# Extra multiplications on TensorE between the phases, and each phase's ScalarE function evaluated once at its head

## The chip, the cores and the metric

The kernel runs on one core of a Trainium2 chip. The metric is the device time of one execution in microseconds: 2099.31 us is the median of three runs before the change (2096.52 to 2101.40).

## The reference

x has 8 batches of 512 tokens with 256 features, all in fp32. Three layers are applied one after the other, each added to x:

```python
x = x + 0.5 * ffn(layernorm(x))
x = x + attn(layernorm(x))
x = x + 0.5 * ffn(layernorm(x))

def ffn(x):                      # the same weights both times
    gf = global_net(mean(x, axis=tokens))       # 256 -> 128 -> 64 -> 1, gelu, gelu, sigmoid
    out = x
    for _ in range(3):
        tf = coupling_net(out)                  # 256 -> 256 -> 128 -> 64 -> 1, three gelu, sigmoid
        coupling = 0.1 + adaptive_range * (0.7 * gf + 0.3 * tf - 0.5) * 2
        out = out + coupling * twist(out)       # [o, p] -> [p, -p, -o, o], by quarters
    return out

def attn(x):                     # 16 heads of 64, and 4 memory keys and values
    q, k, v = x @ Wq, x @ Wk, x @ Wv            # q and k normalised per head
    dots = W_pre_th mixed over heads of (q k^T * 10), causal
    dots = the 64 largest of each row kept, the rest masked
    attn = W_post_th mixed over heads of softmax(dots)
    return (attn @ v * head_scale * sigmoid(x @ Wg + bg)) @ Wo
```

## The kernel before

The program has three phases, each a block in which every engine runs its own list of instructions; the engines meet at the end of a block. Between attention and the second ffn phase stands a fourth part that recomputes a batch if a check asks for it; in this execution it is skipped, and only its flag is read.

**The ffn phase** (`ffn_phase`, L77) runs twice, first with `setup` (it also loads and prepares the weights and makes the identity matrix on GpSimd, L611 and L613), then without it. Its state is kept transposed in SBUF. For each of the 8 batches x is loaded (a DMA on ScalarE's queue in the first phase, L415, on SyncE's in the second, L171 and L175), VectorE normalises it into `xn` (L199 to L214, with GpSimd's power at L277), TensorE turns it with eight transposes (`turn_in`, L285), and ScalarE copies it into the state (`take_in`, L389). Then TensorE works through 24 units (3 cycles of 8 batches) in a loop over 27 steps (L327), in which step k does the first layer of unit k (L342), the second of unit k-1 (L354), and for a pair of units the third (L363) and fourth (L373). `turn_in(k + 2)` stands inside the loop in the first steps. ScalarE evaluates Gelu and Tanh between them, and VectorE updates the state (`update`, four instructions) and at the end adds half of the turned state to x (`add_back`, L248). The state is turned back by `turn_back(b)` (L294, eight transposes at L300); those of batches 0 to 4 stand in the loop, those of 5 to 7 behind it (L380). Each waits for the update of its batch and for the PSUM pair that add_back of batch b-2 frees. In the first phase TensorE then turns the memory keys (`turn_memory`, L711). When add_back of a batch is done SyncE stores the batch, and it waits for all stores before the block ends.

**Attention** (`attention_phase`, L728) treats 32 tiles of 128 tokens, each in 16 groups of 8 rows. Its order on TensorE is written out by hand (L1126 to L1191): `xT(0)` turns the normalised first tile, `tokens` projects q and k (L1008, four calls each), `turn_qk` turns q and then k (L1031), `score` makes the scores (L1049), which ScalarE copies to SC and a DMA brings into `raw`; then the loop over pairs of groups begins with `mix(0)` (L1060) and, for the next tile, `xT(1)` and its q. Before `turn_qk` q and k are squared and copied by ScalarE (L1211, L1214), summed by VectorE (L1525), raised to the power -1/2 by GpSimd (L1411) and scaled by VectorE (L1532). The first `exp` (L1310) comes behind the first steps of that loop.

Every engine's instructions run in the order of the list, and a wait holds back all that stands behind it on that engine.

Of the kernel before, what the change touches and what calls it, by code (L numbers as in the profile page):

```python
# [7 lines left out]
ACT = mybir.ActivationFunctionType  # L8
# [5 lines left out]
P = 128  # L14
# [54 lines left out]
    return -z, step / 2, -step * (counted / 2 - wanted)  # L69


def tiles_of(dram, b):

    return dram[b * N:(b + 1) * N, :].rearrange("(t p) d -> p t d", p=P)


def ffn_phase(nc, tag, X, W, x_dram, out_dram, setup=None, ahead=(), reload=()):  # L77


    with ExitStack() as c:  # L80
        def sb(name, shape):
            return c.enter_context(nc.sbuf_tensor(f"{tag}_{name}", shape, F32))
# [9 lines left out]
        ST = sb("state", [P, 2, B, N])  # L92
        xsum = sb("xsum", [P, 2, B])
        g1 = sb("g1", [P, B])
        g2 = sb("g2", [64, B])
        gth = sb("gth", [P, B])
        offs = sb("offs", [P, B])
# [9 lines left out]
        bank3 = c.enter_context(nc.psum_tensor(f"{tag}_bank3", [P, 512], F32))  # L107
# [175 lines left out]
        def _(pe):  # L283

            def turn_in(b):  # L285
                pe.wait_ge(xn_ready, b + 1)
                wide_free(pe, "x", b)
                for half in range(2):
                    for t in range(TPB):
                        last = nc.tensor.transpose(wide("x", b)[:, half, t * P:(t + 1) * P],  # L290
                                                   xn[b % 2][:, t, half * P:(half + 1) * P], W.ident[:, :])
                last.then_inc(xn_turned, 1)

            def turn_back(b):  # L294
                pe.wait_ge(upd_done, NU - B + b + 1)
                wide_free(pe, "back", b)
                for t in range(TPB):
                    for half in range(2):
                        at = t % 2 * D + half * P
                        last = nc.tensor.transpose(wide("back", b)[:, t // 2, at:at + P],  # L300
                                                   ST[:, half, b, t * P:(t + 1) * P], W.ident[:, :])
                last.then_inc(back_turned, 1)
# [15 lines left out]

            if setup:
                pe.wait_ge(setup.ident_made, 2)  # L320
            turn_in(0)
            turn_in(1)
            if setup:
                pe.wait_ge(setup.ffn_in, 16 * setup.ffn_loads)
# [2 lines left out]
            for k in range(STEPS):  # L327
# [17 lines left out]
                if 0 <= k - 1 < NU:  # L345
# [7 lines left out]
                    for kk in range(2):  # L353
                        last = nc.tensor.matmul(bank2[:, :], W.cn_w2[:, kk, :], h1[u % 2][:, kk, :], start=kk == 0,  # L354
                                                stop=kk == 1)
# [22 lines left out]
                if 0 <= k - (NU - 2) < B:  # L378
                    turn_back(k - (NU - 2))
            for b in range(STEPS - NU + 2, B):  # L380
                turn_back(b)
            if setup:
                pe.wait_ge(h2_ready, NU)
                setup.turn_memory(pe, bank2)

        @block.scalar
        def _(act):

            def take_in(b):  # L389
                act.wait_ge(xn_turned, b + 1)  # L390
                for half in range(2):
                    nc.scalar.activation(ST[:, half, b, :], wide("x", b)[:, half, :], ACT.Identity,
                                         accum_out=xsum[:, half, b:b + 1]).then_inc(state_in, 1)

            def context(h, piece):
                cols = slice(QUAD * h, QUAD * h + QUAD)
                dst, rows, w_bias, scale, func = ((g1, P, W.gc_b1, 1.0 / N, ACT.Gelu), (g2, 64, W.gc_b2, 1.0, ACT.Gelu),
                                                  (gth, P, W.gc_b3h, 0.5, ACT.Tanh))[piece]
                act.wait_ge(g_mm, 3 * h + piece + 1)
                nc.scalar.activation(dst[0:rows, cols], bank2[0:rows, 0:QUAD], func, bias=w_bias[0:rows, 0:1],  # L400
                                     scale=scale).then_inc(g_act, 1)

            def coefficients(pair):
                act.wait_ge(tf_ready, pair + 1)
                act.wait_ge(offs_ready, 1 if 2 * pair % B < QUAD else 2)
                if pair >= 2:
                    act.wait_ge(upd_done, 2 * pair - 2)
                for i in range(2):
                    b = (2 * pair + i) % B
                    nc.scalar.activation(cs[pair % 2][:, i, :], tf[pair % 2][:, i, :], ACT.Identity,  # L410
                                         bias=offs[:, b:b + 1], scale=W.sgn_ar03[:, 0:1]).then_inc(cs_ready, 1)

            if setup:
                for b in range(B):
                    act.dma_start(X[:, b * TPB:(b + 1) * TPB, :], tiles_of(setup.x, b)).then_inc(x_loaded[part_of[b]], 16)  # L415
                setup.store_zeros(act)
            take_in(0)
            take_in(1)
            if setup:
                act.wait_ge(setup.ffn_in, 16 * setup.ffn_loads)  # L420
            for k in range(STEPS):
                if k in G_STEPS:
                    if k == 3 and setup:
                        act.wait_ge(setup.ffn_built, setup.ffn_builds)
                    context(*G_STEPS[k])
                if k < NU:
                    u = k
                    if u >= 2:
                        act.wait_ge(w2_done, u - 1)
                    for m in range(2):  # L430
                        act.wait_ge(w1_done, 2 * u + m + 1)
                        nc.scalar.activation(h1[u % 2][:, m, :], wide("w1", u)[:, m, :], ACT.Gelu,
                                             bias=W.cn_b1[:, m:m + 1]).then_inc(h1_ready, 1)
                if 0 <= k - 1 < NU:
                    u = k - 1
                    if u >= 4:
                        act.wait_ge(w3_done, (u - 4) // 2 + 1)
                    act.wait_ge(w2_done, u + 1)
                    nc.scalar.activation(h2[u % 4][:, :], bank2[:, :], ACT.Gelu, bias=W.cn_b2[:, 0:1]).then_inc(h2_ready, 1)
                if 0 <= k - 2 < NU and k % 2:  # L440
                    pair = (k - 2) // 2
                    if pair >= 2:
                        act.wait_ge(w4_done, pair - 1)
                    act.wait_ge(w3_done, pair + 1)
                    nc.scalar.activation(h3[pair % 2][:, :], bank3[:, :], ACT.Gelu, bias=W.cn_b3[:, 0:1]).then_inc(h3_ready, 1)
                if 0 <= k - 3 < NU and k % 2 == 0:
                    pair = (k - 3) // 2
                    if pair >= 2:
                        act.wait_ge(cs_ready, 2 * pair - 2)
                    act.wait_ge(w4_done, pair + 1)  # L450
                    nc.scalar.activation(tf[pair % 2][:, :, :], pair_out[:, :, :], ACT.Tanh, bias=W.cn_b4h[:, 0:1],  # L451
                                         scale=0.5).then_inc(tf_ready, 1)
                    if pair >= B // 2 - 1:
                        coefficients(pair)
                if k % 2 and 0 <= (k - 5) // 2 < B // 2 - 1:
                    coefficients((k - 5) // 2)
                if k + 2 < B:
                    take_in(k + 2)
            if setup:
                setup.keep_memory(act, bank2)  # L460
# [267 lines left out]
def attention_phase(nc, W, token_weights, a, x_dram, out_dram, again):  # L728

    with ExitStack() as c:  # L730
        def sb(name, shape, dtype=F32):
            return c.enter_context(nc.sbuf_tensor(name, shape, dtype))
# [31 lines left out]
        minus_thr = sb("minus_thr", [P, RING])  # L764
        below = sb("below", [P, RING])
        signs = sb("signs", [P, RING])
        side = sb("side", [P, RING])
        order = sb("order", [P, RING])
        flip = sb("flip", [P, RING], I32)
# [220 lines left out]
        def _(pe):  # L990

            def xT(j):
                def emit():
                    for k in range(2):
                        last = nc.tensor.transpose(bankD[:, 0, k * P:(k + 1) * P], xn[:, k * P:(k + 1) * P], W.ident[:, :])
                    return last
                pe.wait_ge(xn_ready, j + 1)
                pe_use(pe, ("xT", j, 0), emit)
# [116 lines left out]
            def project(t):  # L1115
# [7 lines left out]
                                            stop=q == PAIRS - 1)  # L1123
                last.then_inc(projected, 1)

            xT(0)  # L1126
            tokens(0, "q", Wq)
            tokens(0, "k", Wk)
            turn_qk(0, 0, "qT")
            turn_qk(0, 1, "kT")  # L1130
            for q in range(4):
                score(0, q)
            for n0 in range(0, NG + LAG, 2):
                t, g = divmod(n0, GPT)
                live, ahead = n0 < NG, t + 1 < NT
# [58 lines left out]
        def _(act):  # L1194

            def xT(j):
                if j >= 2:

                    wait_read(act, ("g", j - 2, 1))
                act_use(act, ("xT", j, 0), lambda: nc.scalar.copy(  # L1200
                    xnT[j % 2][:, :, MEM:MEM + P], bankD[:, 0, 0:D].rearrange("p (k n) -> p k n", k=2)))
# [111 lines left out]
            def out_PT(n0):  # L1313
# [14 lines left out]
                    last = nc.scalar.copy(PTtail[0:MEM, :, :], bankT[0:MEM, 0:P].rearrange("p (h i) -> p h i", i=IG))  # L1328
                last.then_inc(PT_out, 2)

            xT(0)
            project_qk(0, 0, "q")
            project_qk(0, 1, "k")
# [1287 lines left out]
```

## Time and profile before

| what | value |
|---|---|
| median of three runs | 2099.31 us |
| the profiled execution | 2098.69 us |
| its span | 2096.9 us |
| mean granted TensorE clock | 0.981 |
| first ffn phase | 0 to about 202 us |
| attention | about 202 to 1894 us |
| second ffn phase | about 1897 us to the end |

In the profile times are microseconds unless marked ns. PE is TensorE's multiplication, PEld its weight load, DVE VectorE, ACT ScalarE, POOL GpSimd, SPq and ACTq the DMA queues of SyncE and ScalarE. L300 is line 300 of the kernel before. PEclk is the granted TensorE clock, in tenths on the page and as a share of full speed in a table of stretches. "x8" counts the records merged into one row. A multiplication is pipelined and its end modelled, so a row can reach a little over the start of the next.

### The profile page before, as it was taken

How to read it: one execution, taken by the hardware profiler on the slowest of the kernel's cores; microseconds unless marked ns; L12 is line 12 of the kernel's file. 1: busy time of each engine (PE TensorE's matmuls, PEld its weight loads, DVE VectorE, ACT ScalarE, POOL GpSimd, SP SyncE). 2: the span in 40 equal slices, each digit the busy share in tenths (PEclk: the TensorE clock that was granted, in tenths of full speed). 3: DMA queues.
4: the chain of work that ended last, by engine and by line, in shares of the span. 5: the costliest groups of instructions: out<-in, count | busy, mean ns of one | idle time of the engine just before them, and what ended most of it. 6: DMA issues, size and time to landing. Idle time of an engine off the chain costs nothing. (4 is left out here: it accounts for less than half of the span.)

```text
span 2096.9 us, 56133 instructions
## 1 busy us (share of the span) xinstructions
PE 1952.4 (93%) x16059; PEld 1292.3 (62%) x16060; DVE 1668.8 (80%) x7716; ACT 1612.7 (77%) x4412; POOL 862.8 (41%) x2675
## 2 busy tenths in 40 slices
PE   7996789999999999999999999999999999996997
PEld 3433456676667666766676677666766776674433
DVE  6355389978997899789978997999699969985335
ACT  4553489978997899789968996899689978963554
POOL 3000454455445544554454445544554455421000
PEclk9997899999999999999999999999999999998998
DMA  5002012301230222122211221122112211213002
GB/s 170 26 1 95 12 33 53 79 18 45 61 73 18 62 55 60 26 54 68 45 33 48 68 48 29 48 68 48 29 48 68 48 26 46 66 45 95 0 1 80
DMA packets 113228, 104.78 MB, mean 50 GB/s; under 512 B 34449, under 2 KB 110865, under 8 KB 112913
## 3 DMA queue, kind: packets, MB, share of 16 engines
q1 hardware_dynamic: 108000, 96.65, 18.6%
q10 hardware_dynamic: 4912, 4.46, 0.7%
q8 instruction: 134, 2.20, 0.5%
q14 instruction: 182, 1.48, 0.2%
HBM read 19.14 MB, written 12.71 MB: 15 GB/s over the span
## 5 line engine op out<-in xcount | busy, mean ns | idle before, releaser
L1076 PEld LDWEIGHTS bankC<-R,E 128*128 128x128 f32 x2560 | 319.9, 192 | 49.7 <-issue 17.6
L1060 PE MATMUL bankB<-raw,mixpre 128*128 128x76 f32 (+37 forms) x1024 | 334.5, 421 | 13.6 <-DMA raw<-SC 12.3
L1076 PE MATMUL bankC<-R,E 128*128 128x128 f32 x2560 | 333.9, 277 | 11.5 <-POOL R L1452 11.5
L1557 DVE TENSOR_SCALAR_CACHE_REDUCE S<-S,minus_thr 128x68 f32<-128x68 f32 (+56 forms) x456 | 232.9, 511 | 110.9 <-POOL minus_thr L1436 110.1
L1427 POOL TENSOR_TENSOR S<-S,diagmask 128x8 f32<-128x8 f32 x512 | 120.2, 238 | 395.4 <-ACT S L1284 360.4
L1284 ACT ACTIVATE S<-bankB,aim_first 128x68 f32<-128x68 f32 (+56 forms) x456 | 227.3, 506 | 57.8 <-PE bankB L1060 56.9
L1452 POOL TENSOR_SCALAR R<-mixpost,rinv 128x128 f32<-128x128 f32 x512 | 199.3, 402 | 101.1 <-DVE rinv L1591 99.0
L1310 ACT ACTIVATE E<-S,nmax 128x12 f32<-128x12 f32 (+56 forms) x512 | 238.8, 523 | 0.0
L1060 PEld LDWEIGHTS bankB<-raw,mixpre 128*128 128x128 f32 x1024 | 160.2, 190 | 119.0 <-issue 94.4
L1646 DVE SCALAR_TENSOR_TENSOR E<-S,limit,E 128x68 f32<-128x68 f32 (+56 forms) x456 | 221.8, 521 | 8.6 <-ACT E L1310 4.7
L1049 PE MATMUL bankD<-KT,QT 64*64 64x132 f32 (+8 forms) x2304 | 177.4, 401 | 43.3 <-ACT qk L1214 29.4
L1102 PEld LDWEIGHTS bankM<-PT,V 128*64 128x64 f32 x5120 | 176.2, 138 | 65.2 <-issue 61.8
L1102 PE MATMUL bankM<-PT,V 128*64 128x64 f32 x5120 | 199.4, 226 | 1.2 <-ACT PTtail L1328 1.2
L1320 ACT COPY PT<-bankC 128x256 f32<-128x256 f32 (+3 forms) x256 | 175.1, 684 | 31.4 <-PE bankT L1082 18.2
L1302 ACT ACTIVATE junk_side<-S 128x68 bf16<-128x68 f32 (+56 forms) x456 | 198.6, 443 | 0.0
L1294 ACT ACTIVATE junk_first<-S 128x60 bf16<-128x60 f32 (+56 forms) x456 | 196.3, 440 | 0.2
L1411 POOL TENSOR_TENSOR rn<-ssq,neghalf 128x16 f32<-128x16 f32 x64 | 190.0, 2969 | 11.3 <-DVE ssq L1526 10.5
L1602 DVE TENSOR_SCALAR near<-S,flip 128x68 int32<-128x68 int32 (+56 forms) x456 | 158.3, 387 | 0.1
L238 DVE TENSOR_TENSOR ffn_mo<-ffn_cs,ffn_state 128x512 f32<-128x512 f32 x48 | 32.9, 686 | 139.3 <-ACT ffn_cs L410 139.3
L1273 ACT COPY SC<-bankD 128x520 f32<-128x520 f32 (+4 forms) x160 | 128.5, 803 | 9.5 <-PE bankD L1049 7.3
L1049 PEld LDWEIGHTS bankD<-KT,QT 64*64 64x64 f32 x2304 | 59.5, 133 | 109.8 <-ACT SC L1273 44.7
L1008 PE MATMUL bankD<-Wq,xnT 128*128 128x512 f32 x256 | 121.8, 620 | 5.0 <-ACT xnT L1200 5.0
(187 smaller groups left out, 4188.7 us busy)
## 6 DMA issues: line engine op xcount, KB each, us to landing
X_first<-in_L_attn_x_dram ACTq DMA_DIRECT2D x8, 512.0 KB, 9.9
x<-X_first SPq DMA_DIRECT2D x8, 512.0 KB, 2.9
xt<-x SPq DMA_DIRECT2D x32, 128.0 KB, 2.4
x<-xt SPq DMA_DIRECT2D x32, 128.0 KB, 2.4
X_last<-x SPq DMA_DIRECT2D x8, 512.0 KB, 7.5
out_dram<-X_last SPq DMA_DIRECT2D x8, 512.0 KB, 2.9
raw<-SC SPq DMA_DIRECT2D x8, 258.0 KB, 5.3
raw<-SC SPq DMA_DIRECT2D x8, 254.0 KB, 4.8
```

The source lines that it names most:

```text
L1049: last = nc.tensor.matmul(bankD[cols, r, i * s[3]:(i + 1) * s[3]], QT[rows, pair, HALF * hh:HALF * hh + HALF], KT[rows, pair, first:first ...
L1060: last = nc.tensor.matmul(bankB[n % 2][:, 0:wide(n)], W.mixpre[:, :], raw[n % RAWS][:, 0:wide(n)], start=True, stop=True)
L1076: last = nc.tensor.matmul(bankC[:, n % 2, jb * P:(jb + 1) * P], E[n % EBUFS][:, jb * P:(jb + 1) * P], R[n % RBUFS][:, :], start=True, stop ...
L1102: last = nc.tensor.matmul(bankM[64 * lo:64 * lo + 64, pair * HALF:(pair + 1) * HALF], V[:, slot(t - blocks + 1 + jb), h * DH:(h + 1) * DH] ...
L1284: nc.scalar.activation(S[n % SBUFS][:, 0:wide(n)], src, ACT.Identity, bias=W.aim_first[:, group(n)]).then_inc(S_out, 1)
L1294: nc.scalar.activation(junk_first[n % 2][:, 0:w], S[n % SBUFS][:, 0:w], ACT.Sign, scale=-1.0, accum_out=below[:, col(n)]).then_inc(below_d ...
L1302: nc.scalar.activation(junk_side[n % 2][:, 0:w], S[n % SBUFS][:, 0:w], ACT.Sign, accum_out=signs[:, col(n)]).then_inc(signs_done, 1)
L1310: nc.scalar.activation(E[n % EBUFS][:, 0:w], S[n % SBUFS][:, 0:w], ACT.Exp, bias=nmax[:, col(n)]) \
L1411: nc.gpsimd.tensor_tensor(rn[:, i, :], ssq[:, i, :], W.neghalf[:, 0:H], ALU.pow).then_inc(rn_ready, 1)
L1452: nc.gpsimd.tensor_scalar(R[n % RBUFS][:, :], W.mixpost[:, :], rinv[:, col(n)], 1.0, ALU.mult, ALU.mult).then_inc(R_ready, 1)
L1557: nc.vector.tensor_scalar(row, row, minus_thr[:, col(n)], None, ALU.add, ALU.max, accum_out=rmax[:, col(n)]).then_inc(max_done, 1)
L1646: at[n] = step(nc.vector.scalar_tensor_tensor(out=E[n % EBUFS][:, 0:w], in0=S[n % SBUFS][:, 0:w], scalar=least, in1=E[n % EBUFS][:, 0:w], ...
```

## The change

A helper `keep_busy(nc, W, bank, times)` is added. It issues `times` multiplications whose weights are the identity matrix (128x128) and whose moving operand is the identity repeated four times (128x512), into a PSUM bank that nothing reads at that point. None of them waits for anything or signals anything. It is called

- in each ffn phase ahead of `turn_in(0)` (7 times in the first, 9 in the second), ahead of `turn_in(1)` (5), ahead of each of the last three `turn_back` (4 each), and in the first phase behind `turn_memory` (8);
- in attention ahead of `xT(0)` (6), between the projection of k and `turn_qk` of q (8), between `turn_qk` of q and of k (5), and between the scores and the loop (4).

ScalarE gets one activation of one column at the head of each phase: Gelu in the ffn phases, Exp in attention. In the first phase it stands between the second and third DMA for x and waits for the identity matrix.

```diff
+def keep_busy(nc, W, bank, times):
+    for _ in range(times):
+        nc.tensor.matmul(bank[:, 0:512], W.ident[:, :], W.ident[:, :].unsqueeze(1).to_broadcast([P, 4, P]), start=True, stop=True)
...
# ffn_phase, TensorE
             if setup:
                 pe.wait_ge(setup.ident_made, 2)
+            keep_busy(nc, W, bank3, 7 if setup else 9)
             turn_in(0)
+            keep_busy(nc, W, bank3, 5)
             turn_in(1)
...
             for b in range(STEPS - NU + 2, B):
+                keep_busy(nc, W, bank3, 4)
                 turn_back(b)
             if setup:
                 pe.wait_ge(h2_ready, NU)
                 setup.turn_memory(pe, bank2)
+                keep_busy(nc, W, bank3, 8)
# ffn_phase, ScalarE
             if setup:
                 for b in range(B):
+                    if b == 2:
+                        act.wait_ge(setup.ident_made, 2)
+                        nc.scalar.activation(primed[:, 0:1], W.ident[:, 0:1], ACT.Gelu)
                     act.dma_start(X[:, b * TPB:(b + 1) * TPB, :], tiles_of(setup.x, b)).then_inc(x_loaded[part_of[b]], 16)
                 setup.store_zeros(act)
+            else:
+                nc.scalar.activation(primed[:, 0:1], W.ident[:, 0:1], ACT.Gelu)
# attention_phase, TensorE
+            keep_busy(nc, W, bankM, 6)
             xT(0)
             tokens(0, "q", Wq)
             tokens(0, "k", Wk)
+            keep_busy(nc, W, bankM, 8)
             turn_qk(0, 0, "qT")
+            keep_busy(nc, W, bankM, 5)
             turn_qk(0, 1, "kT")
             for q in range(4):
                 score(0, q)
+            keep_busy(nc, W, bankM, 4)
             for n0 in range(0, NG + LAG, 2):
# attention_phase, ScalarE
+            nc.scalar.activation(primed[:, 0:1], W.ident[:, 0:1], ACT.Exp)
             xT(0)
```

## Rows read from the trace of the kernel before

**Rows 1.** The page: busy time by engine, and the granted clock in 40 slices.

```profile
PE 1952.4 (93%) x16059; PEld 1292.3 (62%) x16060; DVE 1668.8 (80%) x7716; ACT 1612.7 (77%) x4412; POOL 862.8 (41%) x2675
...
PEclk9997899999999999999999999999999999998998
```

**Rows 2.** Table of stretches: length, busy time (instructions) of each engine, granted clock, DMA.

```profile
220.00:235.00 15.00, 8.30 (x58) 5.89 (x59) 2.47 (x7) 3.47 (x8) 3.78 (x5) 0.56 0.07 12
```

**Rows 3.** Timeline, weight loads of q: start, us, engine, line, operation, [idle before].

```profile
210.24 0.34 PEld L1008 LDWEIGHTS bankD<-Wq,xnT 128*128 128x128 f32 x1 [0.52 <-issue]
211.10 0.34 PEld L1008 LDWEIGHTS bankD<-Wq,xnT 128*128 128x128 f32 x1 [0.52 <-issue]
...
211.77 0.19 PEld L1008 LDWEIGHTS bankD<-Wq,xnT 128*128 128x128 f32 x1 [0.34 <-issue]
```

**Rows 4.** Timeline, TensorE and VectorE at the first ffn phase's end.

```profile
185.08 1.06 PE L300 MATMUL ffn_wide<-ident,ffn_state 128*128 128x128 f32 x8 [1.35 <-DVE X_first L248]
...
194.34 2.34 DVE L248 SCALAR_TENSOR_TENSOR X_first<-ffn_wide,X_first 128x1024 f32<-128x1024 f32 x2
195.70 1.94 PE L300 MATMUL ffn_wide<-ident,ffn_state 128*128 128x128 f32 x8 [1.60 <-DVE X_first L248]
...
197.67 1.22 DVE L248 SCALAR_TENSOR_TENSOR X_first<-ffn_wide,X_first 128x1024 f32<-128x1024 f32 x1 [0.99 <-PE ffn_wide L300]
```

**Rows 5.** Timeline, the first work in attention of VectorE and TensorE.

```profile
202.33 0.17 DVE L1666 COPY KT<-memkT 64x32 f32<-64x32 f32 x1 [3.43 <-PEq L80]
...
206.31 0.69 PE L995 MATMUL bankD<-ident,qksq 128*128 128x128 f32 x2 [8.38 <-DVE qksq L1518]
```

**Rows 6.** Timeline, TensorE at the head of attention.

```profile
207.55 5.67 PE L1008 MATMUL bankD<-Wq,xnT 128*128 128x512 f32 x8 [0.55 <-ACT xnT L1200]
...
213.06 3.60 PE L1008 MATMUL bankD<-Wk,xnT 128*128 128x512 f32 x8
...
219.96 1.09 PE L1031 MATMUL bankD<-ident,qk 128*128 128x128 f32 x8 [3.31 <-DVE qk L1532]
...
224.04 1.97 PE L1031 MATMUL bankD<-ident,qk 128*128 128x128 f32 x8 [2.98 <-DVE qk L1532]
...
226.78 1.18 PE L1049 MATMUL bankD<-KT,QT 64*64 64x68 f32 x32 [0.77 <-ACT KT L1253]
...
230.60 0.57 PE L1060 MATMUL bankB<-raw,mixpre 128*128 128x12 f32 x2 [2.64 <-DMA raw<-SC]
...
232.24 5.27 PE L1008 MATMUL bankD<-Wq,xnT 128*128 128x512 f32 x8 [0.31 <-ACT xnT L1200]
```

**Rows 7.** Timeline, ScalarE and TensorE around attention's table load.

```profile
245.13 1.28 ACT L1310 ACT_TABLE_LOAD   x1
246.42 0.51 ACT L1310 ACTIVATE E<-S,nmax 128x12 f32<-128x12 f32 x2
...
247.15 0.63 PE L1060 MATMUL bankB<-raw,mixpre 128*128 128x60 f32 x4 [1.22 <-ACT S L1287]
```

**Rows 8.** The chain that ended last, where the second ffn phase opens: start, us, what.

```profile
1897.67 4.56 DMA X_last<-x
```

**Rows 9.** Timeline, GpSimd and TensorE at the head of the first ffn phase.

```profile
1.20 0.29 POOL L613 TENSOR_SCALAR_AFFINE_SELECT ident<-ident 128x128 f32<-128x128 f32 x1 [0.24 <-POOL ident L611]
...
10.24 1.94 PE L290 MATMUL ffn_wide<-ident,ffn_xn 128*128 128x128 f32 x8 [10.24 <-DVE ffn_xn L214]
...
22.91 1.09 PE L290 MATMUL ffn_wide<-ident,ffn_xn 128*128 128x128 f32 x8 [0.78 <-DVE ffn_xn L214]
```

**Rows 10.** Timeline, TensorE at the head of the second ffn phase.

```profile
1906.85 1.97 PE L290 MATMUL ffn_wide<-ident,ffn_xn 128*128 128x128 f32 x8 [12.99 <-DVE ffn_xn L214]
...
1911.28 1.97 PE L290 MATMUL ffn_wide<-ident,ffn_xn 128*128 128x128 f32 x8 [2.46 <-DVE ffn_xn L214]
1913.04 4.49 PE L342 MATMUL ffn_wide<-ffn_state,last_cn_w 128*128 128x512 f32 x8
```

More of the change, by code:

```diff
@@ L94, in ffn_phase @@
         g1 = sb("g1", [P, B])
+        primed = sb("primed", [P, 1])
         g2 = sb("g2", [64, B])
@@ L766, in attention_phase @@
         signs = sb("signs", [P, RING])
+        primed = sb("primed", [P, 1])
         side = sb("side", [P, RING])
```

## Prediction

> **What bounds the kernel now.** I read the page first, for engine shares and the granted clock; then a table of stretches over the seams between the phases; then the timeline of each seam; last the weight-load timeline, for what a 128x512 matmul costs at either clock. TensorE is busy 93% of the span, and the reader is to see that its clock is full except in a few slices [rows 1]: the start, the join of the first ffn phase and attention, the join of attention and the second ffn phase, and the end. In the long middles TensorE works without a pause, so a microsecond gained or lost at a seam reaches the end. In the seams it is idle more than it works, and every wait ends with another engine or a DMA. From 220 to 235 us it is busy 8.3 of 15 us at a granted clock of 0.56, mostly the 1.2 GHz level [rows 2]. So two things count at each seam: the duration of what TensorE really does there, and when its operands come.
>
> **What one added multiplication costs.** keep_busy issues 128x128 by 128x512 f32 multiplications. The kernel's own of that shape show two records per call: projecting q is four calls and eight records [rows 6]. At the low clock the records start 0.86 us apart [rows 3]. At the full clock the eight of k take 3.60 us; bundles overlap the next by 0.16 us (q ends at 213.22, k starts at 213.06 [rows 6]), so a record holds the engine 0.43 us. One call is 0.86 us at 2.4 GHz and 1.7 us at 1.2 GHz. Four calls are 3.44 us, five 4.3, six 5.2, eight 6.9. They wait for nothing, but TensorE works in order, so what stands behind them waits until they end. This is the figure on which the forecast hangs: the gaps are 1.6, 2.6, 3.0 and 3.3 us, mostly shorter than their filling.
>
> **End of the first ffn phase.** Four calls stand ahead of the last three turn_backs. The bundle of batch 4 starts at 185.08 [rows 4] and frees TensorE 0.92 us later, 186.0 (1.06 less the overlap). Then follow three fillings and two bundles at the full clock: 186.0 + 3 x 3.44 + 2 x 0.92 = 198.2, where the last bundle started at 195.70 before. It now takes 1.06 instead of 1.94 us and ends at 199.2, not 197.64: 1.6 us later. VectorE waited 0.99 us for it before and nothing else covers it [rows 4]. The two earlier bundles end before VectorE reaches their add_back (the pair starts at 194.34). Then the short turn of mem_k, taken at 0.2 us, and eight calls, 6.9 us, end at 206.2. The phase closed at 202.3 before, with TensorE idle 8.4 us until its first work in attention [rows 5]; the last store, moved by 1.6 us, would be home by 203.9. So the eight calls, not the store, close the phase: attention begins 4.0 us later (3.7 to 4.4).
>
> **Head of attention.** Shifts are against the old start times.
> - Six calls from 206.3 end at 211.5. xT(0) has its operand at 206.31 + 4.0 = 210.3 [rows 5], so it is 5.2 late.
> - At the full clock xT(0) is 0.35 shorter, and q 5.67 - 3.62 = 2.05 shorter [rows 6]. From here the chain through ScalarE, VectorE and GpSimd is 2.8 late.
> - k frees TensorE at 216.5 + 2.8 = 219.3. Eight calls end at 226.2, but qT could start at 219.96 + 2.8 = 222.8. Five more: 227.1 + 4.3 = 231.4, where kT could start at 224.04 + 2.8 = 226.8. So kT is 7.3 late: the filling has become the bound.
> - kT and the scores run at the full clock: 0.8 and 0.45 shorter (the two turns are 1.97 and 1.09 us [rows 6]; for the scores I take four tenths of 1.18). SC and its DMA are 6.05 late, raw lands at 236.7. The last four calls end at 237.4, and mix(0) goes from 230.60 to 237.4: 6.8 late.
> - mix, xT(1) and q(1) are no longer at the low clock: 0.5 and 1.65 off (5.27 against 3.62 [rows 6]). Tile 1 is 4.7 late.
>
> **The table loads.** The Exp load of 1.28 us stands between ScalarE's qk copy and the first exp; TensorE idles 1.22 us for a copy behind it [rows 7]. Priming puts it at attention's head, where ScalarE has no work for microseconds: -1.2. The Trainium skill, ScalarE: Activation LUTs, section "What ACT_TABLE_LOAD costs", gives about 1.28 us for the load and about 1.38 us more for a drain, 2.66 in all. The load agrees [rows 7]; a drain is not seen there, the activation starts 1.29 us after the load does. By the page the gain would be some 2.6 and the total 1.4 better. At the head of the first ffn phase the primed Gelu takes two loads off later work, but six x DMAs on ScalarE's queue are issued about 1.5 us later. ScalarE finishes early enough either way; the second ffn phase's load is hidden beside TensorE. I take 0 for both.
> The slices of the page from 210 to 315 us are not at the full clock either [rows 1], and with the load a gap of TensorE goes that precedes part of this. No row shows what that gives. Bounds are 0 and -3 (a tenth of a slice of 52 us lost is 5 us, some of it beside idle time); I take -0.5, nearest to the 1.22 us gap that goes. Attention's sum: 4.7 - 1.2 - 0.5 = +3.0.
>
> **Head of the first ffn phase.** The identity is there at 1.5 us [rows 9]. Seven calls (14 records) need about 4 us at the low clock and 4 at the full: they end at 9.5, before turn_in(0) at 10.24. The 4 us is what attention shows: q starts at 207.55 [rows 6], and its records, 0.86 us apart up to 211.10, close up to 0.67 by 211.77 [rows 3]. Five calls then reach to 15.5 and turn_in(1) ends at 16.4. The first layer gets 2 us shorter, but behind it turn_in(2) waits for VectorE's xn, which came at 22.9 with TensorE idle 0.78 us already [rows 9]. VectorE's chain starts with the landing of the weights and is not sped up, so the gain becomes idle time: 0. Bounds: -1.5 if the later x DMAs let the weights land earlier, +2 if the clock falls in the 2.9 us of idle time now left.
>
> **Head and end of the second ffn phase.** The block opens at 1897.7, where x's DMA leaves [rows 8]. Nine calls: 4 us low clock (4.7 records), 13.3 records at 0.43, end 1907.4; turn_in(0) was at 1906.85. Five more end at 1912.6; turn_in(1) was at 1911.28 and frees TensorE at 1913.5. The first layer then takes 3.6 instead of 4.49 us and ends at 1917.1 instead of 1917.5 [rows 10]: -0.4, bounds -0.8 and +1. The end of this phase runs the same code on the same four bundles as [rows 4], so its last bundle ends 1.6 later. There no filling follows, the store does: +1.6, bounds +0.7 and +2.
>
> **The sum.** 4.7 - 1.2 - 0.5 - 0.4 + 1.6 = +4.2, on the profiled execution's 2098.69 us (span 2096.9): 2102.9. The median shown, 2099.31, is 0.6 above that execution, so the same sum from there is 2103.5. I forecast 2103, its own range 2100 to 2106.
>
> **Rivals.**
> - **The fillings fit** (the other side). If a call holds TensorE for one record (0.43 us), every filling but the second phase's nine ends inside its gap. Then the last bundles end 0.9 earlier, q and xT give 2.4, kT and scores 1.3, mix to q(1) 2.15, the table load 1.2, and the second ffn phase 0.4 and 0.9: 9.3 in all, 2090. It decides at about 0.6 us a call, where the gap of 3.3 us and the 3.0 behind it no longer hold thirteen calls. For it: the counts look cut to such gaps. Against it: two records per call in each row of that shape.
> - **The delay is absorbed.** Between 250 and 276 us TensorE has idle time, and low-clock stretches may go too. If 3 us of the head's delay vanish there, the time is 2100. Against: what the other engines do there hangs on TensorE's outputs.
> - **The clock is late or falls.** Each further microsecond at 1.2 GHz under fillings costs 0.5 us. If it falls once in the first phase's remaining gap (+2) and rises late in the second (+1), with slower fillings at attention's head (+2), the time is 2108.
>
> **How the numbers follow.** Forecast 0.60, fits 0.08, absorbed 0.18, late clock 0.14. A measurement tells about 0.2% (4.2 us) from no change: below 2095.1 or above 2103.5. The forecast's middle lies at that border: half of it (0.30) is slower, 0.29 the same, 0.01 faster; the late clock gives 0.14 slower; absorbed 0.13 same, 0.05 faster; fits 0.08 faster. That makes 0.14, 0.42, 0.44. The range 2096 to 2109 leaves out the fitting case and the tails.
>
> **What would show it.** Two records of 0.43 us per added call; add_back of batch 7 at 199.2 instead of 197.67; attention's first VectorE work near 206.4; xT(0) at 211.5 following a filling, not VectorE; qT and kT right behind fillings, at 226 and 231; mix(0) near 237.4; no low clock from 186 to 250; no table load near 245; turn_in(2) still at 22.9. The forecast is wrong if a call shows one record, if the phase closes before 205, or if qT and kT still wait for VectorE.

## The result, and the profile after

The changed kernel takes 2106.08 us (median of 9 runs, 2103.56 to 2109.64) against 2098.98 us before (9 runs, 2096.42 to 2101.40): ratio 1.0036, 95% interval 1.0026 to 1.0046. It is 7.1 us slower; the forecast was 2103, 4.2 us slower, with 2096 to 2109 as its range; the median lies just above the narrower 2100 to 2106 that the forecast gave itself. The profiled execution of the changed kernel took 2108.13 us, 2 us above its median, so the parts below add up to 9.4 us and not to 7.1. Of all executions reported below one, of the version with four calls for nine, took 3376.33 us at a mean granted clock of 0.555, and the ratios leave it out.

First the page of the changed kernel: TensorE is busier and its clock is full nearly everywhere, which answers to [rows 1]. The mean granted clock rose from 0.981 to 0.995, and still the span grew by 9.5 us. Busy time is no sign of progress when part of it is filling.

```profile
PE 2009.9 (95%) x16221; PEld 1313.7 (62%) x16222; DVE 1668.2 (79%) x7716; ACT 1611.5 (77%) x4414; POOL 864.5 (41%) x2675
...
PEclk9999999999999999999999999999999999999999
```

The timeline of TensorE at the end of the first ffn phase, changed kernel, against [rows 4, 5] (L75 is a filling, L307 a turn_back, L1012 is xT(0)):

```profile
185.00 1.86 PE L307 MATMUL ffn_wide<-ident,ffn_state 128*128 128x128 f32 x8 [1.35 <-DVE X_first L255]
186.66 4.52 PE L75 MATMUL ffn_bank<-ident 128*128 128x512 f32 x8
191.02 1.04 PE L307 MATMUL ffn_wide<-ident,ffn_state 128*128 128x128 f32 x8
191.89 3.60 PE L75 MATMUL ffn_bank<-ident 128*128 128x512 f32 x8
195.33 1.04 PE L307 MATMUL ffn_wide<-ident,ffn_state 128*128 128x128 f32 x8
196.20 3.60 PE L75 MATMUL ffn_bank<-ident 128*128 128x512 f32 x8
199.63 1.04 PE L307 MATMUL ffn_wide<-ident,ffn_state 128*128 128x128 f32 x8
...
200.80 7.13 PE L75 MATMUL ffn_bank<-ident 128*128 128x512 f32 x16
208.24 5.39 PE L75 MATMUL bankM<-ident 128*128 128x512 f32 x12 [0.30 <-PEq L86]
213.46 0.38 PE L1012 MATMUL bankD<-ident,qksq 128*128 128x128 f32 x2
```

Each four calls show eight records, and 3.60 us at the full clock. After 185.0 no turn_back waits for VectorE any more: each follows a filling at once. The last ends at 200.67 instead of 197.64. The 16 records behind the turn of mem_k end at 207.93, and attention opens at 208.24. One thing is new: the bundle at 185.00 took 1.86 us and the first filling 4.52. The clock had fallen there, before any filling, as the stretches of one microsecond show (the number before the last two is the granted clock):

```profile
184.00:185.00 1.00, 0.00 (x0) 0.03 (x1) 1.00 (x2) 0.97 (x2) 0.00 (x0) 1.00 0.00 0
185.00:186.00 1.00, 1.00 (x5) 1.00 (x6) 1.00 (x3) 1.00 (x2) 0.00 (x0) 0.55 0.14 47
```

The head of attention, changed kernel, against [rows 6] (L1048 turns q and k, L1066 are the scores, L1077 is mix(0)):

```profile
221.34 7.03 PE L75 MATMUL bankM<-ident 128*128 128x512 f32 x16
228.21 1.04 PE L1048 MATMUL bankD<-ident,qk 128*128 128x128 f32 x8
229.08 4.46 PE L75 MATMUL bankM<-ident 128*128 128x512 f32 x10
233.37 1.04 PE L1048 MATMUL bankD<-ident,qk 128*128 128x128 f32 x8
235.23 0.70 PE L1066 MATMUL bankD<-KT,QT 64*64 64x68 f32 x32 [0.82 <-ACT KT L1274]
235.86 3.70 PE L75 MATMUL bankM<-ident 128*128 128x512 f32 x8
239.40 0.29 PE L1077 MATMUL bankB<-raw,mixpre 128*128 128x12 f32 x2
...
240.51 3.67 PE L1025 MATMUL bankD<-Wq,xnT 128*128 128x512 f32 x8 [0.42 <-ACT xnT L1221]
```

The waits of 3.31, 2.98 and 2.64 us of [rows 6] are gone from the rows, but not from the time: what waited now stands behind 7.03, 4.46 and 3.70 us of filling.

The second ffn phase's head, changed kernel, SyncE's queue and TensorE, against [rows 8, 10], and the row of VectorE that makes turn_in(0)'s operand (L1003 stores the last tile of attention):

```profile
1897.81 0.33 SPq L1003 DMA_DIRECT2D x<-xt  x1
...
1901.27 1.85 SPq L178 DMA_DIRECT2D X_last<-x  x2
...
1904.01 10.37 PE L75 MATMUL ffn_bank<-ident 128*128 128x512 f32 x18 [6.56 <-issue]
...
1914.22 1.04 PE L297 MATMUL ffn_wide<-ident,ffn_xn 128*128 128x128 f32 x8
```

```profile
1908.89 1.38 DVE L221 TENSOR_SCALAR ffn_xn<-X_last,ffn_mv,ffn_rstd 128x256 f32<-128x256 f32 x4 [1.14 <-POOL ffn_rstd L284]
```

TensorE's first filling starts 2.74 us behind SyncE's first DMA and waits for nothing that the profile shows ("issue"). VectorE's operand for turn_in(0) was complete at 1910.3; it starts at 1914.22.

The end of the second ffn phase, the bundles of batches 4 and 7: first the kernel before, then the changed kernel.

```profile
2079.72 1.06 PE L300 MATMUL ffn_wide<-ident,ffn_state 128*128 128x128 f32 x8 [1.35 <-DVE X_last L248]
...
2090.34 1.94 PE L300 MATMUL ffn_wide<-ident,ffn_state 128*128 128x128 f32 x8 [1.60 <-DVE X_last L248]
```

```profile
2086.05 1.69 PE L307 MATMUL ffn_wide<-ident,ffn_state 128*128 128x128 f32 x8 [1.35 <-DVE X_last L255]
...
2100.68 1.04 PE L307 MATMUL ffn_wide<-ident,ffn_state 128*128 128x128 f32 x8
```

From the start of the first to the end of the last it was 12.56 us and is 15.67, as in the first phase (185.00 to 200.67). Here too the first bundle is slow (1.69 us) before any filling.

| place | before | forecast | after | shift forecast / measured |
|---|---|---|---|---|
| turn_in(2), first ffn phase | 22.91 | 22.9 | 22.83 | 0 / -0.1 |
| last turn_back ends | 197.64 | 199.2 | 200.67 | +1.6 / +3.0 |
| attention opens (first VectorE work) | 202.33 | 206.3 | 208.24 | +4.0 / +5.9 |
| xT(0) | 206.31 | 211.5 | 213.46 | +5.2 / +7.15 |
| qT | 219.96 | 226.2 | 228.21 | +6.2 / +8.25 |
| kT | 224.04 | 231.4 | 233.37 | +7.3 / +9.3 |
| mix(0) | 230.60 | 237.4 | 239.40 | +6.8 / +8.8 |
| mixing behind the first exp | 247.15 | 250.7 | 252.53 | +3.5 / +5.4 |
| second ffn phase, SyncE's first DMA | 1897.67 | 1900.7 | 1901.27 | +3.0 / +3.6 |
| its first layer of unit 0 ends | 1917.53 | 1920.1 | 1923.86 | +2.6 / +6.3 |
| span | 2096.9 | 2101.1 | 2106.4 | +4.2 / +9.5 |

From attention's opening to mix(0) measured and forecast shifts differ by a constant 1.9 to 2.1 us: that head came out as worked out, only from a later start. The two other steps up are at the head of the second ffn phase (2.7 us where -0.4 was forecast) and at its end (3.1 where 1.6 was). In between, from the mixing behind the first exp to the second phase, the shift shrinks by 1.8 us (5.4 to 3.6) where 0.5 was forecast.

### The profile page after: what moved, and what is told of

It is laid out like the page before. It is cut to its first block and busy times, and to the rows that moved or that the text cites. A ratio compares the mean times of both kernels' runs of the same rounds, so it can differ in the third digit from the quotient of the medians.

```text
span 2106.4 us, 56458 instructions
## 1 busy us (share of the span) xinstructions
PE 2009.9 (95%) x16221; PEld 1313.7 (62%) x16222; DVE 1668.2 (79%) x7716; ACT 1611.5 (77%) x4414; POOL 864.5 (41%) x2675
## 3 DMA queue, kind: packets, MB, share of 16 engines
q10 hardware_dynamic: 4912, 4.46, 0.7%
## 5 line engine op out<-in xcount | busy, mean ns | idle before, releaser
L1077 PE MATMUL bankB<-raw,mixpre 128*128 128x76 f32 (+37 forms) x1024 | 334.0, 421 | 8.5 <-DMA raw<-SC 8.3
L1077 PEld LDWEIGHTS bankB<-raw,mixpre 128*128 128x128 f32 x1024 | 160.0, 190 | 114.4 <-issue 92.1
L1066 PE MATMUL bankD<-KT,QT 64*64 64x132 f32 (+8 forms) x2304 | 177.0, 399 | 43.5 <-ACT qk L1235 29.6
L1433 POOL TENSOR_TENSOR rn<-ssq,neghalf 128x16 f32<-128x16 f32 x64 | 190.0, 2969 | 10.2 <-DVE ssq L1548 9.4
L1066 PEld LDWEIGHTS bankD<-KT,QT 64*64 64x64 f32 x2304 | 59.1, 132 | 109.8 <-ACT SC L1294 44.7
L1455 POOL TENSOR_TENSOR moved<-below,aim_slope 128x2 f32<-128x2 f32 (+1 forms) x232 | 64.9, 280 | 146.1 <-ACT junk_first L1315 146.0
## 6 DMA issues: line engine op xcount, KB each, us to landing
X_first<-in_L_attn_x_dram ACTq DMA_DIRECT2D x8, 512.0 KB, 10.1
```

What stands on the lines that cost most here:

```text
L1066: last = nc.tensor.matmul(bankD[cols, r, i * s[3]:(i + 1) * s[3]], QT[rows, pair, HALF * hh:HALF * hh + HALF], KT[rows, pair, first:first ...
L1077: last = nc.tensor.matmul(bankB[n % 2][:, 0:wide(n)], W.mixpre[:, :], raw[n % RAWS][:, 0:wide(n)], start=True, stop=True)
L1433: nc.gpsimd.tensor_tensor(rn[:, i, :], ssq[:, i, :], W.neghalf[:, 0:H], ALU.pow).then_inc(rn_ready, 1)
```

## Experiments

All times are medians beside runs of the kernel before on the same chip (2098.9 to 2099.2 us).

**Half the columns, all else kept.**

```diff
-        nc.tensor.matmul(bank[:, 0:512], W.ident[:, :], W.ident[:, :].unsqueeze(1).to_broadcast([P, 4, P]), start=True, stop=True)
+        nc.tensor.matmul(bank[:, 0:256], W.ident[:, :], W.ident[:, :].unsqueeze(1).to_broadcast([P, 2, P]), start=True, stop=True)
```

> The changed kernel with every filling at half the columns (the identity twice, 256 columns, instead of four times, 512); the counts of calls stay. Theory (the fillings lose because one call holds TensorE 0.86 us, longer than the gaps it stands in): a call now holds it 0.43 us, all but a few fillings end inside their gaps, and the gains of the full clock stay. From the rows of before: both ends 0.9 less each, q and xT(0) 2.4, kT and scores 1.3, mix to q(1) 2.1, the Exp load 1.2, the head of the second ffn phase 0.4: 9 us faster than before, 2090 us. mix(0) near 226, last bundle of the first ffn phase ending near 196.8. Rival (the loss is not the length, but the clock falling beside the fillings or work that TensorE's idling hid): 2098 to 2104 us.

Measured: 2090.91 us against 2098.92 (ratio 0.9964, 0.9950 to 0.9978), 8.0 us faster than before and 15 us faster than the change. The same 81 calls in the same places, with the same primed activations, win with half their columns. Its timeline at the same places as [rows 4] shows the waits for VectorE back, short ones:

```profile
195.08 1.89 PE L75 MATMUL ffn_bank<-ident 128*128 128x256 f32 x8
197.71 1.06 PE L307 MATMUL ffn_wide<-ident,ffn_state 128*128 128x128 f32 x8 [0.74 <-DVE X_first L255]
...
223.57 1.09 PE L1048 MATMUL bankD<-ident,qk 128*128 128x128 f32 x8 [0.82 <-DVE qk L1554]
...
228.73 0.39 PE L1077 MATMUL bankB<-raw,mixpre 128*128 128x12 f32 x2 [0.62 <-DMA raw<-SC]
```

A wait that is left ahead of the real work, at the full clock, is the sign of a filling that fits. The forecast for mix(0) was 226; it is 228.7, because this execution, the fastest of the five for all that, lost 2 us early on: between the first layer and turn_in(2) TensorE had 2.7 us to wait, the clock fell, and the next first layer took 5.21 us instead of 3.60:

```profile
23.23 1.22 PE L297 MATMUL ffn_wide<-ident,ffn_xn 128*128 128x128 f32 x8 [2.72 <-DVE ffn_xn L221]
24.25 5.21 PE L351 MATMUL ffn_wide<-ffn_state,first_cn_w 128*128 128x512 f32 x8
```

**Only the primed activations.** All calls of keep_busy removed.

> The changed kernel without any filling: only the three primed activations. Theory: the Exp load of 1.28 us leaves the way of the first exp; with what it spares of the low clock behind it 1.2 to 2 us faster than before, 2097.3 us; the two Gelu loads give 0. Rival (six DMAs for x issued later and a later entry into the phases cost as much as the load gives): 2099 us or more.

Measured: 2097.00 us, 1.9 us faster than before (ratio 0.9988, 0.9979 to 0.9997). In its profile the wait of 1.22 us ahead of the mixing of [rows 7] is gone, and the gates of the first tile, which follow it, run at the full clock; first the kernel before, then this one:

```profile
248.62 5.36 PE L1020 MATMUL bankD<-xnT,Wg 128*128 128x128 f32 x32
```

```profile
248.44 3.74 PE L1033 MATMUL bankD<-xnT,Wg 128*128 128x128 f32 x32
```

The 1.22 us are the load's. That the 1.62 us are too is not shown: in attn_head_only and tails_only the load stayed where it was, and the gates took 3.74 us all the same.

**Only the fillings.** The three primed activations removed.

```diff
-                    if b == 2:
-                        act.wait_ge(setup.ident_made, 2)
-                        nc.scalar.activation(primed[:, 0:1], W.ident[:, 0:1], ACT.Gelu)
...
-            else:
-                nc.scalar.activation(primed[:, 0:1], W.ident[:, 0:1], ACT.Gelu)
...
-            nc.scalar.activation(primed[:, 0:1], W.ident[:, 0:1], ACT.Exp)
```

> The changed kernel with all fillings and no primed activation. Theory: the loads go back to where they were; the Exp load costs 1.2 us or a little more, so 2107.3 to 2108 us, 8.5 us over before; the fillings alone carry the loss. Rival (the loss of the change is the priming's, ScalarE entering the phases late with a load): near 2102 us or less.

Measured: 2108.44 us, 9.5 us slower than before (1.0048, 1.0034 to 1.0062). By the medians the fillings lose 9.5 and the priming gives 2.4 of it back; the intervals of the two kernels overlap, so 2.4 is not told from the 1.9 above. In its profiled execution the clock did not fall ahead of the last bundles, and here is the forecast's own case:

```profile
184.81 1.06 PE L307 MATMUL ffn_wide<-ident,ffn_state 128*128 128x128 f32 x8 [1.34 <-DVE X_first L255]
...
197.76 1.04 PE L307 MATMUL ffn_wide<-ident,ffn_state 128*128 128x128 f32 x8
```

From the start of the first to the end of the last it is 13.99 us; before it was 12.56 [rows 4], the forecast 14.1.

**Only the fillings ahead of the last turn_backs.** Those of both ffn phases, nothing else.

```diff
             for b in range(STEPS - NU + 2, B):
+                keep_busy(nc, W, bank3, 4)
                 turn_back(b)
```

> The kernel before with only the fillings ahead of the last three turn_backs of each ffn phase (four calls each, twice three times), nothing else. Theory: 1.6 us later at each end, and up to 1.5 more at each where the clock falls before the first filling as it did in the changed kernel's trace: 3.2 to 6.2 us slower than before, 2102 to 2105 us; last bundles ending 1.6 to 3.1 later than 197.64 and 2092.28. Rival (the ends are covered by the stores that are still under way): within 1 us of before.

Measured: 2101.06 us, 2.1 us slower (1.0010, 1.0001 to 1.0019); less than the 3.2 to 6.2 expected. In its profile, which is of the slowest of the eleven executions (2105.32 us), the four bundles with their fillings took 15.7 us in the first phase, where the clock fell again ahead of them, and 13.99 in the second.

**Only the fillings at the head of attention** (6, 8, 5 and 4 calls).

> The kernel before with only the four fillings at the head of attention (6, 8, 5 and 4 calls of 512 columns), nothing else. Theory (the fillings ahead of qT, kT and mix(0) are longer than their waits): the first filling begins at the low clock and ends near 209.5, xT(0) 3.3 late; q and xT(0) give 2.4 back, kT ends up 5.4 late, mix(0) near 235, and behind the second q, at the full clock, 2.3 us remain, which the 32 tiles carry to the end: 2101.5 us (2100.5 to 2103). Rival (what the full clock gives there pays for the filling): 2099 us or less. Rival (the head's delay is absorbed in the tiles): 2099 us with the gates of the first tile late and those of the last not.

Measured: 2101.48 us, 2.3 us slower (1.0013, 1.0004 to 1.0022), the time that was worked out. xT(0) starts at 209.50, kT at 229.41, mix(0) at 235.43; expected were 209.6, 229.4 and 235. Behind them the profile has two things that were not worked out and that cancel: k of the second tile took 5.37 us instead of 3.67 at 243.03, and the gates of the first tile 3.74 instead of 5.36.

**Only the fillings at the heads of the ffn phases** (7 and 5, 9 and 5 calls).

> The kernel before with only the fillings at the heads of the ffn phases (7 and 5, 9 and 5 calls of 512 columns), nothing else. Theory (TensorE enters the second ffn phase about 2.7 us after SyncE and its nine calls end behind their operand): 2.7 us lost there, and in the first phase 0, or 1.7 where the clock falls in the gap ahead of turn_in(2): 2101.7 to 2103.5 us. Rival (no late entry without the other fillings, as the forecast had it: 0.4 gained): 2098.8 us.

Measured: 2101.45 us, 2.3 us slower (1.0010, 1.0001 to 1.0019), just under the range expected. Its profile, 2 us above that median, shows both losses: the clock falling behind the 2.72 us gap of the first phase (turn_in(2) 1.90 us, first layer 4.51), and TensorE entering the second phase late without any other filling in the kernel:

```profile
1899.93 1.68 SPq L178 DMA_DIRECT2D X_last<-x  x2
...
1902.68 10.21 PE L75 MATMUL ffn_bank<-ident 128*128 128x512 f32 x18 [6.57 <-issue]
```

**Four calls for nine at the second head.** `7 if setup else 9` becomes `7 if setup else 4`.

> The changed kernel with four calls instead of nine at the head of the second ffn phase. Theory (there the filling, begun late, ended 3.9 us behind its operand, which came at 1910.3): eight records at the low clock from 1904.0 end near 1910.5, turn_in(0) starts up to 3.5 us earlier, and 2 to 3.5 us are gained: 2102.6 to 2104.1 us. Rival (VectorE or the x DMAs bound that head, and the filling hides nothing and costs nothing): 2106 us.

Measured: 2103.15 us, 2.9 us less than the changed kernel (1.0017 over before, 1.0007 to 1.0026; the changed kernel's interval begins at 1.0026, so it is a gain, but one of uncertain size). In its profile turn_in(0) starts 8.8 us behind SyncE's first DMA, against 12.95 in the changed kernel. It waits 0.35 us for VectorE there.

**Without the skipped part.** The call of the part that would recompute a batch is removed.

```diff
-        redo_phase(nc, W, token_weights, a, x1_dram, x2_dram, again)
```

> The changed kernel without the part between attention and the second ffn phase that recomputes a batch on a flag and is skipped in this execution; all that runs stays. In the changed kernel's trace TensorE's first filling of the second ffn phase starts 2.74 us after SyncE's first DMA there. Theory (the engines leave the skipped part at different times, TensorE and ScalarE late): without it TensorE's first filling starts within 0.5 us of that DMA, ScalarE's table load too, the three or four microseconds between the two phases shrink, and turn_in(0) waits less for its filling. Rival (TensorE is late for another reason, such as the length of its own list): the distance stays near 2.7 us.

Measured: 2101.14 us, 5 us less than the changed kernel (1.0013 over before, 1.0003 to 1.0023). TensorE and ScalarE now enter the phase with SyncE:

```profile
1899.81 0.32 SPq L1003 DMA_DIRECT2D x<-xt  x1
...
1901.90 0.92 SPq L178 DMA_DIRECT2D X_last<-x  x2
...
1901.90 1.28 ACT L432 ACT_TABLE_LOAD   x1 [12.05 <-PEq L746]
...
1901.94 7.96 PE L75 MATMUL ffn_bank<-ident 128*128 128x512 f32 x18 [2.50 <-PEq L746]
...
1911.97 1.09 PE L297 MATMUL ffn_wide<-ident,ffn_xn 128*128 128x128 f32 x8 [2.07 <-DVE ffn_xn L221]
```

The nine calls fit: 2.07 us are left. So the late entry comes with the skipped part. Not all of the 5 us is the filling's, though: SyncE's own first DMA now comes 2.09 us behind attention's last store instead of 3.46, so 1.4 us go with the skipped part itself, and the kernel before was not run without it. turn_in(0) starts 10.1 us behind that DMA instead of 12.95, 2.9 us less. The DMA table of the stretch around the entry (queue, kind, packets, MB, share) has instruction packets in the changed kernel, as many as in the kernel before:

```profile
q14 instruction: 7, 0.06, 1.6%
q8 instruction: 2, 0.03, 1.0%
```

and without the skipped part only

```profile
q8 instruction: 1, 0.02, 1.3%
```

So program text is brought in there beside x's own transfers. That fetching it makes TensorE late fits, but was not tested by itself.

**Without the eight calls behind turn_memory.**

> The changed kernel without the eight calls behind turn_memory. Theory (they, not the last store, close the first ffn phase: they end at 207.9, the store would be home near 204): attention opens 3.5 to 4 us earlier; the clock may fall in the 3 to 4 us of idle time that are left and the six calls at attention's head then give part of it back: 2102 to 2104.5 us. Rival (the store closes the phase): 2106 us.

Measured: 2106.41 us, nothing gained over the changed kernel (1.0035 over before, 1.0021 to 1.0048). The expectation failed, and its trace says where it went. Attention did open at 205.33 instead of 208.24. But in the 4.49 us of idle time left ahead of it the clock fell, the six calls took 6.82 us, xT(0) came 1.5 us earlier instead of 2.9, and then the clock fell once more, at k of the second tile, so that the second tile's gates start only 0.35 us earlier than in the changed kernel:

```profile
205.33 6.82 PE L75 MATMUL bankM<-ident 128*128 128x512 f32 x12 [4.49 <-PEq L86]
211.99 0.38 PE L1011 MATMUL bankD<-ident,qksq 128*128 128x128 f32 x2
...
245.51 5.37 PE L1024 MATMUL bankD<-Wk,xnT 128*128 128x512 f32 x8 [0.54 <-ACT SC L1289]
```

**Fillings where gaps were left, and counts by the trace.** "fitted" adds two fillings to the version with half the columns; "tuned" then sets counts.

```diff
+                if k == 0 and setup:
+                    keep_busy(nc, W, bank3, 5)
                 if k + 2 < B:
                     turn_in(k + 2)
                 if 0 <= k - (NU - 2) < B:
+                    if k == STEPS - 1:
+                        keep_busy(nc, W, bank3, 2)
                     turn_back(k - (NU - 2))
```

> The changed kernel with fillings of half the columns and two more of them, where the trace of that version still shows gaps: five calls between the first layer of unit 0 and turn_in(2) in the first ffn phase (2.1 us into a gap of 2.7), and two ahead of turn_back of batch 4 (0.85 us into 1.35). Theory (a gap that stays open lets the clock fall behind it: there the first layer of unit 1 took 5.21 us instead of 3.60 and the phase's end came 2 us late): the clock stays full through the first phase, 1.5 to 2 us faster than half_width, 2089 us. Rival (the fall near 24 us was chance and the added calls give nothing): 2091 us or more.

Measured: 2091.49 us (0.9966, 0.9954 to 0.9979), no better than half_width. The first phase did what was expected (first layer of unit 1 in 3.60 us, first mixing of attention at 227.03 instead of 228.73), but by the gates of the second tile both executions stood 8.6 us ahead of before: the 1.7 us had gone again, most of it at the third tile's q, which took 5.19 us at 264.42 and only 3.60 in half_width.

> The version 'fitted' with counts set by the idle time its trace still shows, all calls of 256 columns: 8 for 7 at the head of the first ffn phase, 4 for 9 at that of the second (TensorE enters late there), 5 for 4 ahead of the last turn_backs (0.75 us open), 11 for 8 behind turn_memory and 8 for 6 at attention's head (1.48 and 1.39 open), 6 for 5 ahead of kT (0.82), 5 for 4 ahead of mix(0) (0.63). Theory (each filling still ends before its operand, and the shorter one at the second phase's head frees turn_in(0) that was up to 2.5 us late there): 2089 to 2090.5 us. Rival (what is left varies with where the clock falls in the first tiles of attention, and no count changes it): 2090.5 to 2092 us, as half_width and fitted.

Measured: 2090.25 us (0.9959, 0.9945 to 0.9973), 8.9 us faster than before: the lowest median of all, but not to be told from half_width. In its profile TensorE paused inside the first filling of the second phase, again waiting for nothing shown:

```profile
1892.87 0.80 PE L75 MATMUL ffn_bank<-ident 128*128 128x256 f32 x1 [6.57 <-issue]
1897.49 3.15 PE L75 MATMUL ffn_bank<-ident 128*128 128x256 f32 x7 [3.82 <-issue]
```

## Why the prediction was right in its direction and small in its size

**The price of a call** was right: two records of 0.43 us, from the kernel's own rows of that shape. It carried the forecast, and half_width shows it from the other side: halving it alone turned +7.1 into -8.0 us. The rival "the fillings fit" had the counts right and the length wrong; its 2090 us is what that kernel took.

**The head of attention** was right in its chain: +2.3 by itself with every start within 0.5 us, and in the full change every start from xT(0) to mix(0) at the forecast's distance from the opening.

**The head of the first ffn phase** was right: turn_in(2) still waits for VectorE at 22.8, so its shorter first layer gives nothing. The seven calls took 9.27 us where 8 were counted, and turn_in(0) started at 10.65 instead of 10.24, which vanished in the same wait. The bound of +2 for a falling clock there came true in five of the seven profiled executions that have fillings ahead of turn_in(2) and leave the gap behind them open (half_width, ffn_heads_only, no_end_8, no_redo and head_9_to_4: 4.5 to 5.3 us for the next first layer instead of 3.60), not in those of the change and of no_priming. So the 0 of that term was in part luck.

**Priming** was taken at 1.7 with its side effects and measured 1.9 alone and 2.4 under the fillings. The slices of [rows 1] can't show what the forecast read from them, since 9 stands for 90% and more; a table of stretches can: the granted clock before was 0.82 from 210 to 262 us and 0.94 from 262 to 315.

**The step that failed** is "The block opens at 1897.7, where x's DMA leaves [rows 8]." and the end of the nine calls that was counted from it, 1907.4. I took the moment at which one engine starts in a block for that of all. TensorE starts 2.7 us later, and only while the skipped part stands between the phases. The row of before could not show it, because TensorE had nothing to do before 1906.85 [rows 10]. The calls were also slower than counted: turn_in(0) starts 10.2 us behind the first of them, not 9.7, so more of them ran at the low clock than was taken from attention's head. The term measured +2.7 instead of -0.4 in the change's profile; head_9_to_4 gives 2.9 us back and no_redo removes the lateness.

**Both ends** were mis-sized in the profiled execution, not in mechanism: +3.0 and +3.1 instead of +1.6. Where the clock held (no_priming, and tails_only in the second phase) the four bundles took 13.99 us against 14.1 forecast. Where it fell ahead of them, after gaps of 0.35 and 1.35 us with 1.1 us of work between them, it was 15.67 us, so the fall cost 1.7 us more. The forecast assumed that filling behind the first bundle keeps the clock, but nothing fills the gap ahead of it. It fell ahead of the first phase's last bundles in four of the six profiled executions with 512 columns there (the change, tails_only, no_redo, head_9_to_4) and ahead of the second's in two (the change, no_redo), so the change's profile, with both, is on the slow side.

**"The delay is absorbed"** did not come true. The gates of the second tile start 4.2 us later than before, those of the last 3.6 later; in half_width those of the second 8.6 us earlier. From the second tile on, the tiles carry on what the head gives or takes within 0.8 us (in half_width the gates of the last tile start 9.4 us earlier). The first tile does not: there the shift shrank from 5.4 to 4.2 us, since its gates took 3.74 us instead of 5.36. That is the term of -0.5, and it measured -1.2.

The parts measured alone are +2.1 (ends), +2.3 (attention's head), +2.3 (ffn heads) and -1.9 (priming), 4.8 of 7.1. Each of them has an interval of about 1.9 us to either side, so the 2.3 us that are left over are not told from nothing. The eight calls that close the first phase were never run alone, and without them nothing was gained, because the clock fell in other places. That split stays open.

**The rival "the clock is late or falls"** gave 2108 us, and the profiled execution took 2108.13, but not by its terms. It wanted a fall in the first phase's remaining gap and slower fillings at attention's head; the first layer behind that gap took 3.60 us and the six calls 5.39, both at the full clock. What fell was the clock at the two ends.

## What to carry to other kernels

A filling costs nothing only while it ends before the operand of what stands behind it; price one call from a row of the same shape, in both records, and keep the sum below the wait that the trace shows, leaving some wait open. Take the start of a filling from the engine that issues it, not from another engine's first instruction, above all behind code that is skipped. A risen mean clock and a busier TensorE are no gain in themselves: here both went with 7 us more and, with half the columns, with 8 us less.

## What was not expected of the hardware

TensorE and ScalarE began a phase 2.7 and 3.3 us later than SyncE (1904.01 and 1904.54 against 1901.27), with no wait shown, and within 0.04 us of it when the skipped part of the program was gone. The clock fell ahead of bundles after gaps of 1.35 and 2.7 us in some executions and not in others in which the same instructions stand there (184.8 to 188: no_priming kept it, tails_only lost it in the first phase and kept it in the second). What decides it, no run here shows. The granted clock reads 1.00 in the first microseconds, though the seven calls there took 9.27 us instead of the 6.2 of the full clock.
